# Plain attention of 16 narrow heads: one head at a time, or quads of heads in 32-row tiles of TensorE

## The reference

```
q, k, v = [split_heads(h @ W + b) for W, b in ...]        # h: the normalised row; 16 heads of 8
scores = einsum('bhqd,bhkd->bhqk', q, k) / sqrt(8)
scores = where(causal, scores, -10000.0)                  # first layer only; the later one has no mask
probs = softmax(scores)
x = x + einsum('bhqk,bhkd->bhqd', probs, v).reshape(b, s, d) @ Wo + bo
```

## Time and profile before

| what | value |
|---|---|
| median of 3 runs | 6488.11 us (6483.91 to 6490.93) |
| the profiled execution | 6496.69 us, its span 6494.9 us |
| PE busy | 5702.8 us, 88% of the span |
| DVE, ACT, POOL busy | 4375.9, 4302.4, 2324.8 us |
| first plain attention | 13.9 to 309.1 us |
| second plain attention | 5881.9 to 6215.8 us |
| mean granted clock of TensorE | 0.951 |

### The profile page before, as it was taken

How to read it: one execution, slowest core, us unless ns; L and a number is a source line. 1 busy time by engine, 2 the same in 40 slices (tenths; PEclk the granted TensorE clock), 3 DMA queues, 4 the chain that set the end, 5 groups by cost and what they waited for, 6 DMA issues and landing times. The chain is left out here.

```text
span 6494.9 us, 123906 instructions
## 1 busy us (share of the span) xinstructions
PE 5702.8 (88%) x41922; PEld 4234.5 (65%) x41922; DVE 4375.9 (67%) x17032; ACT 4302.4 (66%) x13318; POOL 2324.8 (36%) x1802
## 2 busy tenths in 40 slices
PE   8885699999999999995599999999999997778989
PEld 7774466666666666664366666666666665666778
DVE  4453677777777777773577777777777775444432
ACT  5511587777777777772377777777777774445643
POOL 0000455454545454550354554545454541000000
PEclk9996799999999999996699999999999998889999
DMA  0000000000000000000000000000000000000000
GB/s 10 20 1 3 20 1 14 6 11 9 11 9 2 14 6 11 8 1 3 20 1 11 9 11 9 1 14 6 11 9 11 8 1 5 1 1 3 1 27 7
DMA packets 30976, 53.58 MB, mean 8 GB/s; under 512 B 7688, under 2 KB 17168, under 8 KB 29712
## 3 DMA queue, kind: packets, MB, share of 16 engines
q1 hardware_dynamic: 30352, 45.66, 2.3%
HBM read 44.60 MB, written 1.05 MB: 7 GB/s over the span
## 5 line engine op out<-in xcount | busy, mean ns | idle before, releaser
L1707 POOL TENSOR_TENSOR turnA<-raw,ropes 128x512 f32<-128x512 f32 x768 | 968.7, 1272 | 1291.4 <-ACT raw L1754 1249.0
L1542 PE MATMUL bank<-wA,next_rowT 128*128 128x512 f32 x2304 | 1188.6, 625 | 241.2 <-DVE turnB L1874 151.9
L1730 ACT ACTIVATE pairs<-pairs,negmax 128x128 f32<-128x128 f32 (+1 forms) x3072 | 1239.8, 420 | 19.0 <-DVE negmax L1835 15.6
L1835 DVE CUSTOM_DVE_ANT_0 pairs<-bank,bands,big 128x128 f32<-128x128 f32 (+1 forms) x3072 | 941.8, 362 | 90.8 <-PE bank L1471 87.2
L1714 POOL TENSOR_TENSOR qk<-turnA,turnB 128x512 f32<-128x512 f32 x768 | 967.5, 1270 | 0.0
L1542 PEld LDWEIGHTS bank<-wA,next_rowT 128*128 128x128 f32 x2304 | 378.3, 190 | 688.2 <-DVE turnB L1874 366.6
L1737 ACT ACTIVATE pairsT<-bank 128x512 f32<-128x512 f32 x768 | 468.8, 610 | 343.6 <-PE bank L1484 343.4
L1720 POOL TENSOR_TENSOR qk<-qk,big 128x1024 f32<-128x1024 f32 x192 | 365.6, 1904 | 913.7 <-DVE recip L1949 913.7
L251 POOL TENSOR_TENSOR rstd<-vareps,neg_half 128x2 f32<-128x2 f32 x56 | 39.0, 697 | 1794.1 <-DVE vareps L240 1794.1
L1730 ACT ACTIVATION_READ_ACCUMULATOR pairs<-pairs,negmax 128x1 f32 x3072 | 629.0, 205 | 0.0
L1874 DVE TENSOR_TENSOR turnB<-bank,ropes 128x512 f32<-128x512 f32 x768 | 522.9, 681 | 0.0
(11 more groups left out here) (271 smaller groups left out, 12152.6 us busy)
## 6 DMA issues: line engine op xcount, KB each, us to landing
wA<-in_wt_wqkv SPq DMA_DIRECT2D x72, 256.0 KB, 2.8
wB<-in_wt_wo SPq DMA_DIRECT2D x12, 512.0 KB, 3.6
wC<-in_wt_w SPq DMA_DIRECT2D x12, 341.0 KB, 2.9
wD<-in_wt_w SPq DMA_DIRECT2D x12, 192.0 KB, 2.4
big<-in_e_up SPq DMA_DIRECT2D x1, 2048.0 KB
big<-in_e_down SPq DMA_DIRECT2D x1, 2048.0 KB
scl<-in_wt_scales SPq DMA_DIRECT2D x12, 128.0 KB, 3.1
X<-in_x SPq DMA_DIRECT2D x8, 128.0 KB, 2.4
```

What stands on the lines that cost most here:

```text
L1542: pe.matmul(side_bank(i)[:, :], c.next_rowT[:, t * P:(t + 1) * P], wqkv[:, k * 512:(k + 1) * 512], start=True, stop=True).then_inc(s.chunk ...
L1707: g.tensor_tensor(c.turnA[:, m % 2, :].rearrange("p (h d) -> p h d", h=8), c.raw[:, m % 4, :].rearrange("p (h d) -> p h d", h=8), cos, ALU ...
L1730: last = a.activation(tile, tile, ACT.Exp, scale=-1.0, bias=c.negmax[:, 2 * p + side, t:t + 1], accum_out=c.pair_sums[:, p % 4, t, side:si ...
L1835: last = v.tensor_tensor_reduce(c.pairs[:, 2 * (p % 4) + side, AT[t]:AT[t] + SPAN[t]], c.bank[side][:, AT[t]:AT[t] + SPAN[t]], c.bands[:, ...
```

## The change

`plain_attention` uses a new class `QuadHeads`; the latent attention keeps `NarrowHeads`.

- Heads in quads: quad j has the heads j, 4 + j, 8 + j, 12 + j, one in each 32 partitions. One pick on DVE keeps a quad's queries (4 in place of 16 a row). Products take 32 rows of the array each, a head's own strip.
- Scores are computed twice. `scores` puts two heads' scores in banks 0 and 1 (8 units a row), only for the maxima: `take_max` reduces both banks at once. The 16 x 256 negated maxima are turned by PE (`turn_maxima`) and copied by ACT. `flipped` computes the scores of a quad transposed, keys on the partitions, in banks 4 to 7, and adds to each the negated maximum of its query by a second product, whose weights (`chosen`) pick the head's row. ACT takes one exponential over four heads (`exp`), and the result is already in the form that the weighting reads.
- `weigh` gives each head of a quad 32 of the 128 output rows: values by probabilities in the left half of bank 2, a block of ones by probabilities in the right half, which yields the sums in the place of each output. `finish` divides.
- Rows run as a pipeline: turn b of the loop holds the flipped scores and weightings of row b, the scores and maxima of row b + 1, norm and projections of row b + 2, and the output of row b - 1. Projections, transpositions, values and output share bank 3. Loops run over 11 turns for 8 rows.
- The last weighting of a row, `weigh(b, 3)`, stands at the end of the turn, behind `maxima(b + 1)`.
- PSUM is one tensor of 4096 columns, whose eighths are the banks. The expert layers share semaphores.

```diff
-    c.bank = [ctx.enter_context(nc.psum_tensor(f"bank{i}", [P, 512], F32)) for i in range(8)]
+    c.psum = ctx.enter_context(nc.psum_tensor("bank", [P, 4096], F32))
+    c.bank = [c.psum[:, 512 * i:512 * (i + 1)] for i in range(8)]
+    c.pick, c.chosen, c.ones = sb("pick", [P, 4]), sb("chosen", [P, 4]), sb("ones", [P, 4, 32])
...
+class QuadHeads:
...
+        picks = (flat[0][:, 0:1024], flat[0][:, 1024:2048], flat[1][:, 0:1024])
+        self.picks = [x.rearrange("p (j s) -> p j s", j=4) for x in picks]
+        self.maxima = flat[1][:, 1024:1280]
+        self.negT = (flat[1][:, 1280:1536], flat[1][:, 1536:1792])
...
+        self.recips, self.ctxn = flat[1][:, 1792:2048], c.next_rowT[:, :]
+        self.probs = [x.rearrange("p (i s) -> p i s", i=4) for x in flat[2:4]]
...
+    def scores(self, pe, turn, a):
+        c, j, u = self.c, a // 2, a % 2
+        pe.wait_ge(self.picked, turn * 4 + j + 1)
+        if a == 0:
+            pe.wait_ge(self.k_ready, turn + 1)
+        if turn * 8 + a > self.before * 8:
+            pe.wait_ge(self.max_ready, turn * 8 + a)
+        for t in range(HALVES):
+            for i in (2 * u, 2 * u + 1):
+                rows = slice(32 * i, 32 * i + 32)
+                last = pe.matmul(c.bank[i % 2][:, self.at[t]:self.at[t] + self.span[t]],
+                                 self.picks[turn % 3][rows, j, t * P:(t + 1) * P], self.kT(turn)[rows, 0:self.span[t]],
+                                 start=t == 0, stop=not self.causal, skip_group_check=True)
+        if self.causal:
+            for t in range(HALVES):
+                for i in range(2):
+                    end = self.at[t] + self.span[t]
+                    last = pe.matmul(c.bank[i][:, end - P:end], c.identb[:, :], c.causal[:, :], start=False, stop=True,
+                                     skip_group_check=True)
+        last.then_inc(self.scores_ready, 1)
+    def turn_maxima(self, pe, turn, out):
+        pe.wait_ge(self.max_ready, (turn + 1) * 8)
+        for t in range(HALVES):
+            last = pe.transpose(out[:, t * P:(t + 1) * P], self.maxima[:, t * P:(t + 1) * P], self.c.ident[:, :])
+        last.then_inc(self.neg_in_psum, 1)
+    def flipped(self, pe, turn, j):
+        c, neg = self.c, self.negT[turn % 2]
+        if j == 0:
+            pe.wait_ge(self.neg_ready, turn + 1)
+        if turn * 4 + j > self.before * 4:
+            pe.wait_ge(self.exp_ready, turn * 4 + j)
+        for kt in range(HALVES):
+            q0 = self.q0[kt]
+            for i in range(4):
+                rows = slice(32 * i, 32 * i + 32)
+                pe.matmul(c.bank[4 + i][:, S * kt:S * kt + S - q0], self.kT(turn)[rows, kt * P:(kt + 1) * P],
+                          self.picks[turn % 3][rows, j, q0:S], start=kt == 0, stop=False, skip_group_check=True)
+            for i in range(4):
+                rows = slice(32 * i, 32 * i + 32)
+                last = pe.matmul(c.bank[4 + i][:, S * kt:S * kt + S - q0], c.chosen[rows, j:j + 1].broadcast_to((32, P)),
+                                 neg[rows, q0:S], start=False, stop=not self.causal, skip_group_check=True)
+        if self.causal:
+            for kt in range(HALVES):
+                for i in range(4):
+                    last = pe.matmul(c.bank[4 + i][:, S * kt:S * kt + P], c.causal[:, :], c.identb[:, :], start=False,
+                                     stop=True, skip_group_check=True)
+        last.then_inc(self.flipped_ready, 1)
+    def weigh(self, pe, turn, j):
+        c, probs = self.c, self.probs[j % 2]
+        pe.wait_ge(self.exp_ready, turn * 4 + j + 1)
+        if j == 0:
+            pe.wait_ge(self.v_ready, turn + 1)
+            if turn > self.before:
+                pe.wait_ge(self.ctx_ready, turn)
+        for kt in range(HALVES):
+            q0 = self.q0[kt]
+            first, final = j == 0 and kt == 0, j == 3 and kt == 1
+            for i in range(4):
+                pe.matmul(c.bank[2][32 * i:32 * i + 32, q0:S], self.head_values(turn, kt, i, j),
+                          probs[:, i, S * kt:S * kt + S - q0], start=first, stop=final, skip_group_check=True)
+            for i in range(4):
+                last = pe.matmul(c.bank[2][32 * i:32 * i + 32, S + q0:2 * S], c.ones[:, j, :],
+                                 probs[:, i, S * kt:S * kt + S - q0], start=False, stop=final, skip_group_check=True)
+        last.then_inc(self.weighed, 1)
+    def pick(self, v, turn):
+        for j in range(4):
+            v.tensor_scalar(self.picks[turn % 3][:, j, :], self.q, self.c.pick[:, j:j + 1], None,
+                            ALU.mult).then_inc(self.picked, 1)
+    def take_max(self, v, turn, a):
+        c, j, u = self.c, a // 2, a % 2
+        v.wait_ge(self.scores_ready, turn * 8 + a + 1)
+        out = self.maxima.rearrange("p (t i r) -> p i t r", t=HALVES, i=4)[:, 2 * u:2 * u + 2, :, j]
+        both = c.psum[:, 0:1024].rearrange("p (i s) -> p i s", i=2)
+        if self.causal:
+            for t in range(HALVES):
+                last = v.tensor_reduce(out[:, :, t], both[:, :, self.at[t]:self.at[t] + self.span[t]], AX, ALU.max, negate=True)
+        else:
+            last = v.tensor_reduce(out, both.rearrange("p i (t k) -> p i t k", t=HALVES), AX, ALU.max, negate=True)
+        last.then_inc(self.max_ready, 1)
+    def finish(self, v, turn):
+        c = self.c
+        v.wait_ge(self.weighed, (turn + 1) * 4)
+        v.reciprocal(self.recips, c.bank[2][:, S:2 * S]).then_inc(self.recip_ready, 1)
+        v.wait_ge(self.recip_ready, turn + 1)
+        v.tensor_tensor(self.ctxn, c.bank[2][:, 0:S], self.recips, ALU.mult).then_inc(self.ctx_ready, 1)
+    def exp(self, a, turn, j):
+        a.wait_ge(self.flipped_ready, turn * 4 + j + 1)
+        if turn * 4 + j - 1 > self.before * 4:
+            a.wait_ge(self.weighed, turn * 4 + j - 1)
+        scores = self.c.psum[:, 2048:4096].rearrange("p (i s) -> p i s", i=4)
+        a.activation(self.probs[j % 2][:, :, 0:self.width], scores[:, :, 0:self.width], ACT.Exp).then_inc(self.exp_ready, 1)
...
+            def turn_row(b):
+                if ok(b - 2):
+                    pe.wait_ge(core.neg_ready, core.before + b - 1)
+                elif ok(b - 1):
+                    pe.wait_ge(core.v_ready, core.before + b)
+                norm.transpose(pe, b)
...
+            def maxima(b):
+                if ok(b + 1):
+                    pe.wait_ge(core.v_ready, core.before + b + 2)
+                else:
+                    pe.wait_ge(added, before + b - 1)
+                core.turn_maxima(pe, core.before + b, side)
...
+            for b in range(-2, B + 1):
+                if ok(b + 2):
+                    turn_row(b + 2)
+                flipped(b, 0)
+                scores(b + 1, 0)
+                scores(b + 1, 1)
+                if ok(b + 2):
+                    project(b + 2)
+                flipped(b, 1)
+                scores(b + 1, 2)
+                weigh(b, 0)
+                scores(b + 1, 3)
+                if ok(b - 1):
+                    out(b - 1)
+                flipped(b, 2)
+                scores(b + 1, 4)
+                weigh(b, 1)
+                scores(b + 1, 5)
+                if ok(b + 2):
+                    values(b + 2)
+                scores(b + 1, 6)
+                flipped(b, 3)
+                scores(b + 1, 7)
+                weigh(b, 2)
+                if ok(b + 1):
+                    maxima(b + 1)
+                weigh(b, 3)
...
+            for b in range(-2, B + 1):
+                if ok(b + 2):
+                    norm.scalar(a, b + 2)
+                if ok(b):
+                    core.exp(a, core.before + b, 0)
+                if ok(b + 2):
+                    copy_qk(b + 2)
+                for j in range(1, 4):
+                    if ok(b):
+                        core.exp(a, core.before + b, j)
+                if ok(b + 1):
+                    core.copy_maxima(a, core.before + b + 1, side[:, 0:S])
...
+            for b in range(-2, B + 1):
+                take_max(b + 1, 0)
+                if ok(b - 1):
+                    core.finish(v, core.before + b - 1)
+                take_max(b + 1, 1, 2, 3)
+                if ok(b - 1):
+                    add(b - 1)
+                take_max(b + 1, 4, 5)
+                if ok(b + 3):
+                    norm.statistics(v, b + 3, step)
+                if ok(b + 2):
+                    spread(b + 2)
+                take_max(b + 1, 6)
+                if ok(b + 3):
+                    norm.normalise(v, b + 3)
+                take_max(b + 1, 7)
+                if ok(b + 2):
+                    v.wait_ge(q_ready, before + b + 3)
+                    core.pick(v, core.before + b + 2)
```

(16 more changed lines are left out.)

203 lines of the change are left out of this document (138 added, 65 removed).

## The result

The changed kernel takes **6388.5 us** (median of 4 runs, 6385.94 to 6392.44) against 6489.0 for the kernel before (4 runs, one more than in the table of before); the ratio is 0.9847, 95% interval 0.983 to 0.9864. That is a gain of 100.5 us. The forecast was 6370 and a gain of 118, with 6325 to 6435 as its range. The profiled execution has a span of 6384.2 us.

A forecast was written before the change was run, and what follows sets the result against it. TensorE was taken to bound both attentions; filling, turns and draining summed to 257 and 254 us, gains of 38 and 80, together 118, taking the median from 6488.1 to 6370 us; range 6325 to 6435.

The forecast's parts named there:

- I take the second, since the nearest row loses nothing: PE's four-tile streams: four tiles run for the price of one, so flipped scores cost 5.2 us a causal row.
- Rival A: PE: each group of four tiles pays a start of 0.1 us, 51 us in all, time 6421; chance 0.11.
- Rival B: PE's instruction feed: 61 ns a pass is a floor, adding 55 us, time 6425; chance 0.09.
- Rival C: PE: four tiles run only two at a time, adding 195 us, time 6565, slower; chance 0.08.
- D: Scores: every unit turns into a round trip to DVE, so the time does not change; chance 0.02.
- The rule of the Trainium skill: Four-tile streams: measured speedup 3.07, not 4, for four row tiles; by it 59 us more, time 6429.
- Shape changes: PE: changing tile shape costs 0.18 us, 30 times a causal row for 5.4 us, 15 times unmasked for 2.7.
- clock 0.5 in the filling and 1.00 after: Sign of being right: PE's clock at 0.5 while row 0 fills the pipeline, 1.00 in the rows after.
- bare waits: PE waits for DVE's maxima at two uncovered places a row, 1.3 and 0.8 us, together 2.1 (2.4 unmasked).
- The draining: Stage end: four quads at 3.9 us (4.2 unmasked), then 5.5 (5.7) for last weighting, division, output and addition.
- The filling: Stage start: 9 us to the first pick, then row 0's eight units, 27 us (26.5 unmasked) at 1.2 GHz.
- The place of the last weighting: Turn's end: it covers ACT's copy of the maxima; priced at nothing, without it some 0.7 us a row.

The follow-up runs named there:

- the one-tile run: Changed kernel with all eight products of a half in column tile 0, in the second to fourth weighting of each row; 6606.3 us (one run).
- the run with the busy filling: Changed kernel with three more unread whole-array products of 256 columns behind each of row 0's eight units of scores; 6381.2 us (one run).
- The run with covered units: Changed kernel with PE's order altered so flipped scores or a weighting stand between any two units of scores; 6346.8 us (4 runs).
- the two later kernels in that order: Changed kernel with units covered and row 0 on two bank pairs, 6329.7 us; the same with 14 unread products ahead of row 0, 6329.4 us.
- the run with both edits: Changed kernel with units of scores covered and row 0's units alternating between banks 0, 1 and 4, 5; 6329.7 us (5 runs).
- the warm-up: 14 unread products of 256 columns ahead of row 0: 6329.4 us on the kernel with both edits, 6392.6 us on the changed kernel alone.

## Why the prediction was right, and where it was off

**Right: the sign, the range, the mechanism.** Four tiles run for the price of one; without that overlap, in three of four weightings alone, the time is 6606.3. The step "I take the second, since the nearest row loses nothing" held: 0.43 us for four products, and the factor of 4.0 from the one-tile run. Rival A needed 0.1 us exposed in each of the 32 groups of four: groups of 256 columns step 0.43 us, no more than one product of them alone, and only the first behind an entry into 32-row tiles takes that 0.1, which in a row is four such groups and the eight units. It is the 0.20 that A saw in the earlier trace rows: 0.11 for the change and 0.1 for the entry. Rival B needed 61 ns a pass: 27 were measured. Rival C needed weightings of 2.6 us: they take 1.44. D, no change, fell too. The rule of the Trainium skill (TensorE: Matmul & The Clock Gate, Part 3), 3.07 for four row tiles, does not hold in this stream, where both row and column tiles reach 4; and the 62 ns per MATMUL that its Part 1 names for decoding in software is not the pace here (27 ns).

**The turn came out right by three errors that nearly cancel.** Shape changes were taken at 0.18 us, worked out as what was left of a row of half-array tiles; they are 0.11 to 0.12, which is 30 x 0.07 = 2.1 us a causal turn too much. Against that, the 12 entries into 32-row tiles cost 0.1 more each, 1.2 us a turn; and the rest, some 0.3, lies in projections, values, output and transpositions, which step longer than their columns give. The stream is 26.0 for 26.6, the waits 2.2 for 2.1. In the unmasked turn it is 26.1 for 25.7, and 1.9 for 2.4.

**The step that failed: "clock 0.5 in the filling and 1.00 after".** It was taken from the earlier trace rows. The prediction added 2.1 us of bare waits a turn, priced them by their length, and named "the clock falling within steady rows" as a sign to look for, but put no price on it. Each dip costs 1.6 us (29.8 - 28.2). In the turns of the first attention dips cost 7.9 us: 1.6 twice, and 4.7 in the last turn, where 28.2 less 1.2 for row 8 were due. In the second they cost 3.3. The slow end of the filling adds 4.2 and 3.9 us in the first turns (31.0 and 29.7, where the run with the busy filling has 26.8 and 25.8). That is 19 us together, where 21 were missed in the stages; the sum had nothing for either. The run with covered units shows that the waits are needed for a dip: the same work without them has none in any steady turn, nor have the two later kernels in that order, and the runs that keep the waits keep the dips.

But waits alone are not the cause. PE of the kernel before, at the end of a row of the second attention:

```profile
6051.41 0.71 PE L629 MATMUL bank<-wB,ctxT 128*128 128x128 f32 x4 [1.00 <-DVE ctxT L554]
...
6054.37 1.97 PE L471 MATMUL bank<-kT,qT 128*128 128x256 f32 x8 [0.94 <-DVE qT L524]
6057.37 0.66 PE L484 MATMUL bank<-ident,pairs 128*128 128x128 f32 x4 [1.04 <-ACT pairs L562]
```

It waited 21.0 us in the seven rows, 3.0 a row, and the changed kernel waits 1.9 a turn by the same view; yet the clock was 1.00 in both windows of the earlier trace rows. What else a dip takes was not tried: the longer single wait (1.21 and 1.42 us in place of at most 1.04), or the 32-row and 32-column tiles around it. So that part of the cause stays open.

**The draining looks short by one piece, and is not.** The sum let the four quads of row 7 begin with the turn of the maxima. By this very change the last weighting of row 6 stands behind it: first flipped scores at 259.58, 1.8 us behind 257.78, and 2.2 in the second attention. But the sum had that weighting among its seven turns, while the first turn as measured has none, so 1.4 and 1.9 us only lie on the other side of the cut. What the drainings are short by is 0.3 and 1.8 us, 1.5 of it a dip. The quads themselves take 3.7 and 4.0 us against 3.9 and 4.2; the second one also holds the output of row 6, which the sum left out (4.2 us, and 6.1 with the dip). The last turn, which prepares no row 8, saved 1.2 us rather than 2 (24.8 against 26.0 in the covered run).

**The filling was right** (37.4 and 38.2 for 37 and 36.5): 3.4 us a unit at half clock, as measured. Its 2.5 at full clock was never seen with the wait in it; 2.53 is a unit with PE kept busy.

**The place of the last weighting** is worth 0.4 us a turn; "nothing" for the change as made was right, since the copy of the maxima is covered in all turns but the first (0.5 us), and the worth of that cover was put too high.

In sum: 21 us of stage time were missed, about 17 in the turns, 2 in the drainings, 2 in the fillings; 13 us outside the two stages came as a gain in the profiled executions, which no step explains. That is luck: the stretch between the two attentions takes 5559.4 us in this run and 5568.4 in the run with the busy filling, the same program there, and 5572.8 before. One figure of the prediction is a slip of the pen: the profiled execution with the change was to take 6496.7 - 118 = 6378.7 us, not 6579; the 6370 follows from 6378.7. It took 6385.9, which is 7.2 more: about 21 less 13. The other 11 of the 18.5 us between 6370 and 6388.5 are the place of the profiled executions among their runs: 8.6 above the median before, 2.5 below it after.

## What to carry to other kernels

When a change leaves bare waits in TensorE's stream, price the wait and then ask what the clock does, and do not take the answer from another stream with waits of about 1 us: here 2.2 us of waits a turn cost about 3.7 in the first attention (1.9 and 2.6 in the second), where the kernel before had waited more and kept its clock. The cheapest cure was order alone: independent work between every producer and the next user of its buffer, 42 us, and a second buffer where the pipeline fills and other banks lie idle, some 17 more. No turn had a dip once nothing was waited for. For narrow heads, four 32-row or 32-column tiles are worth their full factor, and a change of tile shape costs about as much as 64 columns (0.11 us), into 32-row tiles about twice that, so group by shape.

## What the hardware showed that was not expected

- Dips in steady rows come in some turns and not in others with the same waits, often in every second one (clean turns 28.2, dipped 29.8, and one of 31.7). What decides which turn dips was not tried, nor why the waits of the kernel before brought none.
- Row 0 of the first attention, on two pairs of banks, streams without a wait from one unit to the next and stays at half clock (1.58 us for the scores, at 31.66 and again at 33.78), while whole-array products in the same place lift the clock within the filling (unit of 2.53 us). In the second attention the unmasked tiled scores do reach full speed in that run, but not in the run with both edits. Whether tiles, masks or the stretch before make the difference stays open.
- The 14 products of the warm-up do lift the clock, but it is lost again before row 0, behind four waits of 0.5 to 1.2 us.
- Two units of scores in different tiles and banks, with no whole-array product between, run beside each other unasked: 2.03 us for both at half clock, where one takes 2.0.
- The reciprocal of 256 elements from PSUM takes 1.75 us on DVE, where a product of as many takes 0.42.
